# ScalarE writes the masks of units 1 to 30 into the scores' banks; even steps weight first

## The reference

```python
scores = einsum('bhqd,bhkd->bhqk', q, k)
if causal:
    scores = where(triu(ones, k=1), -inf, scores)      # layer 1 of 3
scores = where(padding_mask[:, None, None, :], scores, -inf)
attn = nan_to_num(softmax(scores / sqrt(64)))
out = einsum('bhqk,bhkd->bhqd', attn, v)  # then @ wo + bo, + residual, layer norm
```

## Time and profile before

| | |
|---|---|
| time, median of 3 runs | 516.41 us (515.79 to 516.68) |
| the profiled execution, its time | 516.77 us |
| its span, first to last instruction | 515.0 us |
| busy: TensorE, VectorE, ScalarE, GpSimd | 97%, 84%, 70%, 61% of the span |
| granted TensorE clock | 1.00 throughout |
| unit 0's mask product, unit 31's | at 12.1 us and 319.8 us |

### The profile page before, as it was taken

How to read it: one execution, slowest core, us unless ns; L and a number is a source line. 1 busy time by engine, 2 the same in 40 slices (tenths; PEclk the granted TensorE clock), 3 DMA queues, 4 the chain that set the end, 5 groups by cost and what they waited for, 6 DMA issues and landing times.

```text
span 515.0 us, 23708 instructions
## 1 busy us (share of the span) xinstructions
PE 499.9 (97%) x10308; PEld 465.2 (90%) x10308; DVE 431.5 (84%) x762; ACT 361.2 (70%) x988; POOL 312.8 (61%) x611
## 2 busy tenths in 40 slices
PE   8999999999999999999999999899999999999985
PEld 7889999999999999999999997789999999999975
DVE  4988999888899788787878779888889888888874
ACT  6666756757867667756767585868778887888761
POOL 2627566455458454454644338878777887887825
PEclk9999999999999999999999999999999999999999
DMA  8920000000021010000000000000000000000000
GB/s 230 339 96 13 3 13 13 13 3 14 3 84 43 6 41 3 3 3 3 3 3 2 3 3 3 1 4 3 3 9 11 13 8 10 14 8 9 9 8 24
DMA packets 10183, 13.80 MB, mean 27 GB/s; under 512 B 864, under 2 KB 7392, under 8 KB 10080
## 3 DMA queue, kind: packets, MB, share of 16 engines
q1 hardware_dynamic: 10080, 12.28, 7.5%
HBM read 11.23 MB, written 1.05 MB: 24 GB/s over the span
## 4 chain that ended last, share of the span: by engine, by line
PE 89%; DVE 5%; ACT 2%; issue 1%; POOL 1%; POOLq 0%; DVEq 0%; ACTq 0%
PE ps_p L699 16%; PE ps_p L530 10%; PE ps_p L531 9%; PE ps_p L532 9%; PE ps_p L665 8%; PE ps_a L584 5%; PE ps_a L606 5%; PE ps_p L654 5%; PE ps_a L562 4%; PE ps_p L656 4%; PE ps_p L655 4%; PE ps_p L606 3%; PE ps_p L721 2%; DVE turn L929 2%; PE ps_a L573 2%
## 5 line engine op out<-in xcount | busy, mean ns | idle before, releaser
L699 PE MATMUL ps_p<-wo,headsT 128*128 128x128 f32 x768 | 94.1, 276 | 1.8 <-DVE headsT L937 0.9
L1223 POOL TENSOR_TENSOR small<-mv,epsilon 128x1 f32<-128x1 f32 x48 | 10.4, 216 | 139.1 <-DVE mv L958 139.1
L699 PEld LDWEIGHTS ps_p<-wo,headsT 128*128 128x128 f32 x768 | 90.4, 192 | 3.6 <-ACT headsT L764 1.0
L774 ACT ACTIVATE vv<-ps_p 128x512 f32<-128x512 f32 x96 | 56.9, 610 | 50.4 <-PE ps_p L656 47.1
L929 DVE TENSOR_TENSOR turn<-ps_p,rope 128x1024 f32<-128x1024 f32 x64 | 76.2, 1221 | 11.4 <-PE ps_p L532 9.5
L530 PE MATMUL ps_p<-xT_hi,wq_hi 128*128 128x256 f32 x192 | 59.1, 308 | 0.5 <-issue 0.2
L810 ACT ACTIVATE probs<-ps_a,top 128x64 f32<-128x64 f32 x256 | 55.8, 351 | 5.1 <-DVE top L1002 2.8
L1032 DVE TENSOR_REDUCE total<-probs 128x16 f32<-128x1024 f32 x48 | 58.1, 1211 | 0.2
L782 ACT ACTIVATE qT<-ps_p,columns 128x256 f32<-128x256 f32 x126 | 49.3, 495 | 10.5 <-PE ps_p L532 10.2
L1006 DVE TENSOR_REDUCE top<-ps_a 128x8 f32<-128x512 f32 x64 | 41.1, 683 | 16.7 <-PE ps_a L584 16.6
L531 PE MATMUL ps_p<-xT_lo,wq_hi 128*128 128x256 f32 x192 | 54.5, 284 | 0.0
(11 more groups left out here) (148 smaller groups left out, 1380.9 us busy)
## 6 DMA issues: line engine op xcount, KB each, us to landing
out<-y_out SPq DMA_DIRECT2D x16, 64.0 KB, 1.5
raw<-in_x_turned SPq DMA_DIRECT2D x1, 768.0 KB, 10.4
across<-in_across SPq DMA_DIRECT2D x1, 704.0 KB, 8.3
raw<-in_ctx_turned SPq DMA_DIRECT2D x5, 128.0 KB, 2.3
wq_raw<-in_L_xattn_sa_wq SPq DMA_DIRECT2D x2, 256.0 KB, 2.9
wk_raw<-in_L_xattn_sa_wk SPq DMA_DIRECT2D x2, 256.0 KB, 4.4
wv_raw<-in_L_xattn_sa_wv SPq DMA_DIRECT2D x1, 512.0 KB, 7.4
wo<-in_L_xattn_sa_wo SPq DMA_DIRECT2D x1, 512.0 KB, 8.3
```

The costliest lines, as they stand in the source:

```text
L699: last = mm(bank[:, 0:E], headsT[:, p, :, :].rearrange("r b q -> r (b q)"), wo[:, layer % 2, p, :], start=(p == 0), stop=(p == PAIRS - 1))
L774: ins = nc.scalar.activation(vv[:, u % 2, j, :, :].rearrange("k p d -> k (p d)"), bank[:, :], ACT.Copy)
```

## The change

- For units 1 to 30 (`masked_by_scalar`) the mask product on TensorE is gone. ScalarE writes the mask into the two score banks in the step before, by `put_masks`: two copies of 128x512, each after VectorE's shift of that bank. `scores` waits for them (`masked`) and adds to what is there. Units 0 and 31 keep the product.
- On ScalarE `heads_out` goes from behind the exponentials to the front of the step, ahead of T, FT and V. `put_masks(u + 1)` stands behind the exponentials.
- In even steps from 2 to 30 TensorE does the weighting ahead of the scores.
- Each half of the partitions now holds the masks of its own sequence first: `mask_u8` is loaded by two DMAs of 64 partitions from an array with both orders. `keys_at_all` is one reduction of 128 partitions in place of two of 64. The masks of units 4 to 15 are made in steps 1 and 2 in place of 2 and 3.

```diff
...
@@ -92,6 +92,11 @@
 
+def masked_by_scalar(u):
+
+    return 0 < u < 2 * UNITS - 1
+
+
 def turned_by(u):
@@ -164,6 +169,7 @@
 SHIFTED = Tally(lambda u: [(0,), (1,)] if attends(u) and not by_head(u) else [])
+MASKED_BANK = Tally(lambda u: [(0,), (1,)] if masked_by_scalar(u + 1) else [])
 EXPED = Tally(lambda u: [(0,), (1,)] if attends(u) else [])
@@ -422,8 +430,8 @@
         READY = 4
-        FIRST_MASKED, FIRST_VALID, MASKED, FOLD = 2, 5, 7, 23
-        VALID = {4: (0, slice(4, 10), 10), 5: (0, slice(10, 16), 13), 6: (1, slice(0, 8), 16), 7: (1, slice(8, 16), 19)}
+        FIRST_MASKED, FIRST_VALID, MASKED, FOLD = 2, 4, 6, 18
+        VALID = {4: (0, slice(4, 10), 8), 5: (0, slice(10, 16), 10), 6: (1, slice(0, 8), 12), 7: (1, slice(8, 16), 14)}
 
@@ -477,8 +485,8 @@
             sp.dma_start(columns[:, :], a["columns"]).then_inc(first_loaded, 16)
-            sp.dma_start(mask_u8[:, :, :, :], a["mask_BxS2_bf1"].rearrange("(u b) k -> u b k", b=2).partition_broadcast(128))\
-              .then_inc(mask_loaded, 16)
+            for b in range(2):
+                sp.dma_start(mask_u8[64 * b:64 * b + 64, :, :, :], a["masks"][b].partition_broadcast(64)).then_inc(mask_loaded, 16)
             sp.dma_start(w_raw[2][:, :], weight(0, "v")).then_inc(w_loaded[2], 16)
@@ -548,7 +556,8 @@
                             of = slice(32 * i, 32 * i + 32)
-                            m = mask[of, 1, u % UNITS, b:b + 1, :]
+                            own = (i // 2) ^ b
+                            m = mask[of, 1, u % UNITS, own:own + 1, :]
                             mm(ps_a[64 * b:64 * b + 64, i ^ b, 0:256], fold[of, :], m.broadcast_to([32, 4, S]),
@@ -566,12 +575,16 @@
 
-                for h in range(2):
-                    for b in range(2):
-                        of = slice(64 * h, 64 * h + 64)
-                        m = mask[of, 0 if layer == 0 else 1, u % UNITS, b:b + 1, :]
-                        mm(ps_a[64 * b:64 * b + 64, h ^ b, :], eye_bf[of, of], m.broadcast_to([64, 8, S]),
-                           start=True, stop=False, skip_group_check=True)
+
+                if masked_by_scalar(u):
+                    pe.wait_ge(masked, MASKED_BANK.at(u - 1, 1))
+                else:
+                    for h in range(2):
+                        for b in range(2):
+                            of = slice(64 * h, 64 * h + 64)
+                            m = mask[of, 0 if layer == 0 else 1, u % UNITS, h ^ b:(h ^ b) + 1, :]
+                            mm(ps_a[64 * b:64 * b + 64, h ^ b, :], eye_bf[of, of], m.broadcast_to([64, 8, S]),
+                               start=True, stop=False, skip_group_check=True)
 
@@ -738,12 +751,16 @@
                     pe.wait_ge(setup_dve, MASKED if u else FIRST_MASKED)
-                if attends(u) and u != N - 1:
+
+                late = u % 2 == 0 and masked_by_scalar(u)
+                if attends(u) and u != N - 1 and not late:
                     scores(u)
                 if u - 1 in BIAS_STEPS:
                     pe.wait_ge(bvwo_read, BIAS_STEPS.index(u - 1) + 1)
                 if finishes(u) and not heads_in_ring(u):
                     weight_values(u)
+                if late:
+                    scores(u)
                 for at, (name, j, _) in enumerate(fills(u)):
@@ -819,6 +836,14 @@
 
+            def put_masks(u):
+
+                act.wait_ge(setup_dve, FIRST_MASKED if u < READY else MASKED)
+                m = mask[:, u // UNITS, u % UNITS, 0:1, :].broadcast_to([128, PAIRS, S])
+                for j in range(2):
+                    act.wait_ge(shifted, SHIFTED.at(u - 1, j))
+                    nc.scalar.activation(ps_a[:, j, :].rearrange("q (p k) -> q p k", k=S), m, ACT.Copy).then_inc(masked, 1)
+
             def normalise_rest(u):
@@ -876,13 +901,15 @@
                     act.wait_ge(first_loaded, 16)
+                if finishes(u) and not heads_in_ring(u):
+                    heads_out(u)
                 for at, name, j in ahead:
                     empty(u, at, name, j)
                 if attends(u):
                     for j in range(2):
                         exponentials(u, j)
-                if finishes(u) and not heads_in_ring(u):
-                    heads_out(u)
+                if masked_by_scalar(u + 1):
+                    put_masks(u + 1)
                 for at, name, j in behind:
@@ -1076,9 +1103,7 @@
                 dve.wait_ge(setup_dve, masked)
-                for b in range(2):
-                    of = slice(64 * b, 64 * b + 64)
-                    V.tensor_reduce(valid[of, kind, units], mask[of, kind, units, b, :], AX_X, ALU.max).then_inc(setup_dve, 1)
+                V.tensor_reduce(valid[:, kind, units], mask[:, kind, units, 0, :], AX_X, ALU.max).then_inc(setup_dve, 1)
                 dve.wait_ge(setup_dve, count - 1)
@@ -1087,9 +1112,9 @@
                     keys_at_all(0, slice(0, READY), FIRST_MASKED, FIRST_VALID)
+                elif u == 1:
+                    masks(slice(READY, UNITS))
                 elif u == 2:
-                    masks(slice(READY, UNITS))
-                elif u == 3:
                     causal_masks(slice(READY, UNITS), MASKED - 1)
@@ -1101,7 +1126,7 @@
             def before_m1():
-                dve.wait_ge(mask_loaded, 16)
+                dve.wait_ge(mask_loaded, 32)
                 dve.wait_ge(setup_pool, CAUSAL)
@@ -1331,7 +1356,9 @@
     arrays = {name: np.ascontiguousarray(inputs[name]) for name in _INS}
-    arrays["mask_BxS2_bf1"] = arrays["mask_BxS2_bf1"].view(np.uint8)
+    masks = arrays.pop("mask_BxS2_bf1").view(np.uint8).reshape(UNITS, 2, S)
+
+    arrays["masks"] = np.ascontiguousarray(np.stack([masks, masks[:, ::-1, :]]))
 
...
```

More of the change, by code:

```diff
@@ L396, in build @@
         exped = sem("exped")
+        masked = sem("masked")
         normed = sem("normed")
```

## The result

The changed kernel takes 513.93 us (median of 20 runs, 512.76 to 516.41), the kernel before 516.62 us (20 runs): a ratio of 0.9944, 95% interval 0.9928 to 0.9959. That is 2.7 us less, where 4.9 were forecast; the range of 509.4 to 514.4 holds it. The profiled execution has a span of 511.6 us against 515.0.

What follows compares the result with a forecast made beforehand. TensorE, busy 97% of the span, was taken as the bound. Gains and losses by step summed to 4.9 us, so 516.41 - 4.9 = 511.5 us (forecast 510.6 to 512.3), with a range of 509.4 to 514.4.

Steps and rivals of the forecast that it cites:

- What bounds the kernel, what is removed: TensorE's stream, busy 97%, bounds the span; thirty units lose a mask product of 0.24 us each, 7.2 us as ceiling.
- Even steps: Weighting ahead of scores: VectorE's slip costs nothing, 0.1 us a step as other bound; each gives its 0.24 us.
- The mask pair: Two added ScalarE mask copies per unit, SBUF into PSUM: 0.95 to 1.04 us of queue, taken as 0.95.
- Rival A: Mask copies cost d more queue than the head copies; gain 4.1 us at d = 0.1, 2.9 at 0.2; chance 0.20.
- Odd steps without FFN: Steps 3 to 19: 0.16 us of margin at the output projection's ring bank; each gives 0.24 us.
- Odd steps with FFN: Steps 21 to 29: first hidden bank frees no earlier, so each of five gives 0.09 of the 0.24 us.
- The start: Steps 0 to 2: added mask copies delay the bias copy the weighting waits for; TensorE 0.65 us late.
- Step 6: The weighting waits for the bias copy's end: 0.43 us of stall; with the step before it, 0.06 us gained.
- Step 30: Output projection waits 0.80 us for VectorE; the 0.24 us only lengthen that wait, so gain nothing.
- C: The first score itself pays the mask's 0.24 us, so nothing is saved: 516.4 to 517.4; no measurable change 0.10.
- D: Nothing lost at the start, FFN steps keep their full 0.24: gain 6.7, 509.7 us; chance 0.14 with what lies between.
- B: Mask copies far slower: gain gone at d = 0.37, 2.2 us slower (518.6) at d = 0.5; chance 0.06.

Runs made afterwards that it cites:

- the run without the order: Changed kernel with ScalarE still writing the masks, but scores ahead of the weighting in every step: 517.48 us, ratio 1.0013 to the kernel before.
- the shifted kernel: Changed kernel with 32 small matmuls in place of two of the start's eight identity matmuls: 517.27 us, ratio 1.0014 to the kernel before.

## Why the prediction was right in its range and wrong in its parts

**What bounds the kernel, what is removed.** Right. TensorE is busy for 97% as before, and units gave time wherever nothing else came late. Even steps gave 0.22 to 0.23 of the 0.24, odd ones 0.16 to 0.20: there the scores take 0.06 us more up to the weighting than behind a mask product. That the product in flight ahead of them made the difference is a reading; no run isolates it.

**The mask pair.** Taken as 0.95 us of queue, measured 1.04 to 1.05, the upper bound. The instruction is as short (586 ns) as the head copy it was compared with (596); its successor starts later. The Trainium skill (ScalarE: Activation LUTs, What ACT_TABLE_LOAD costs) gave 1.04 as an estimate, and the trace agrees. Rival A's mechanism with d = 0.09 is what happened, but its price at 0.1 is a gain of 4.1 us, not 2.7.

**Odd steps without FFN.** Right: 0.16 us of margin were claimed with a pair of 0.95, the longer pair used 0.1 of it and still fits, and the run with another pair lost 1.02 us of 1.04 a step.

**Odd steps with FFN.** The step that failed most: 0.09 us to be gained each, 0.42 lost in the fills. The chain was right, down to the bank; three of its terms were too small. The head copies start 2.16 us behind the first score, not 208.94 - 206.89 = 2.05; the mask pair is 0.09 longer; the rest is 0.04. So the first hidden copy, taken to stand where it stood, comes at 211.80 - 205.01 = 6.79 us against 213.44 - 206.89 = 6.55. The margin of 0.09 turned into a wait of 0.3 us. With rival A's "d each after the 0.09 is gone" the loss was still counted too low, since the late start of the head copies was in no term. Masks last in these steps: 1.7 us back.

**The start.** The order of the waits was right, and in the first profile the loss was smaller than feared: 0.33 us at unit 2, 0.65 forecast. What the prediction lacked is the clock. It counted the wait at its length; in six of seven executions a stretch at half the clock followed, which cost 1 to 2 us. With the wait filled with matmuls, and with the wait cut to 1.2 us, every run of five kept a mean clock of 0.999 or more and the spread fell to 0.7 and 0.3 us, from 1.9 and more; of the changed kernel's own 25 runs 16 kept it. So standing still is a part of the cause.

**Step 6.** Forecast 0.43 us of stall less 0.24 of gain, measured +0.80. Steps 5 and 6 after, GpSimd, TensorE, ScalarE; the bias copy (L920) answers the earlier trace rows:

```profile
62.01 3.17 POOL L1235 TENSOR_TENSOR turn<-turn 128x512 f32<-128x512 f32 x3
65.23 0.49 PE L741 MATMUL ps_a<-turn,valid 128*128 128x128 f32 x2 [0.26 <-POOL turn L1235]
65.76 0.28 ACT L920 ACTIVATE bvwo<-ps_a 128x128 f32<-128x128 f32 x1 [0.69 <-PE ps_a L741]
66.09 1.16 PE L619 MATMUL ps_a<-probsT,vv 64*64 64x64 f32 x64 [0.37 <-ACT bvwo L920]
```

Three sums on GpSimd took 3.17 us and end after TensorE's fills, so the bias product itself waits. That term was in no sum: of the 0.80 us, 0.42 had come before the bias product started (65.23 against 65.09, in a stream that was 0.28 ahead), and 0.38 behind it, where 0.19 was forecast. Before, the three took 2.62 us, and 2.63 in the run without the order. The third alone differs, 0.99 against 0.45, and in all twelve profiles where it takes 0.99 VectorE's normalising starts 0.01 to 0.02 us ahead of it:

```profile
64.17 1.55 DVE L1074 TENSOR_TENSOR probs<-probs,rinv 128x512 f32<-128x512 f32 x2
```

In the other two VectorE is at a reduction then, since a small instruction before it (128x6; L1083 before, L1108 after) took 1.04 and 1.25 us in place of 0.27, and normalises only when the third sum is done. That the two engines hold each other up is what these rows suggest; no run isolates it.

**Even steps.** Right: the added work is hidden there, nearly twice over. **Step 16:** right, unit 17 came 0.57 us earlier with the late projection gone. **Step 30:** right that it gains nothing, wrong that its wait grows: it is 0.51 us in the first profile after and 0.80 in the second, as before.

**Rivals.** C fell (even steps gave nearly their 0.24), D fell, B's price was not reached. A came true in mechanism. The time, 513.93 us, is outside the forecast's own 510.6 to 512.3 and in A's 512.3 to 514, but not for A's reason alone. None of them had the clock or the gaps.

**The sum.** Up to unit 31 the changed kernel was 1.4 us ahead in its profile, where 4.9 were forecast. The missing 3.5 are the FFN steps (1.4), step 6 (0.7), two gaps (0.82 + 0.43) and 0.5 in small parts, less 0.3 that the start did better. 1.4 us of gap near the end of the kernel before were not there after, and 0.2 at unit 34 and 0.36 at unit 44, not followed up, came with them. So the measured 2.7 us are partly the change and partly where 256-record boundaries fell, and that they lie within the range is in part luck.

## What to carry to other kernels

Price an instruction that is added to a queue by the distance from start to start, with the upper bound where the rows differ, and put it behind the last thing that another engine waits for: the same copies cost 0.42 us a step ahead of the FFN's hidden layer and nothing behind the key copies. Where two orders are possible, measure each half of a change, and look for gaps before you put a loss down to it: here the copies alone and the order alone were no faster, both together gave 2.7 us, and both, with the masks placed by step and the old order in step 6, 5.8. Count a stall of TensorE at more than its length, for the clock may fall behind it.

## What the hardware showed that was not expected

- A wait of 2.3 us of TensorE (the 1.9 of the expectations) was followed by a granted clock of 0.50 for 3.4 us in six of seven profiled executions, at a cost of 1 to 2 us; the fall came between 0.4 us before the end of the wait and 1.2 behind it. With one wait of 0.8 to 1.2 us in that place, or with matmuls in the wait, it stayed at 1.00. It also fell behind three waits that make 1.8 us together, and stayed at 1.00 once behind the wait of 2.3 us and once, without the new order, behind 2.2 us on keys. So the length of one wait doesn't decide it, and what does was not found.
- TensorE's instructions come in packets of 256 records, and behind none of 1122 did the next record start within 1.18 us of the landing. Where the 256 before are worked off quickly, in 2.6 us in step 10, the engine can stand still for up to 1.5 us at the boundary. Moving code by a few dozen records, 56 in the shifted kernel, changes where it happens, and the same kernel has it in one execution and hardly in another (0.82 and 0.24 us).
- Three GpSimd sums took 2.6 or 3.2 us by what VectorE did beside them: the third took 0.99 us in place of 0.45 whenever VectorE's normalising had started just before it.
